# In every fourth step, half of the row maxima come from a + relu(b - a)

## Time and profile before

| | us |
|---|---|
| median of 3 runs (3239.01 to 3239.97) | 3239.01 |
| the profiled execution | 3237.97 |
| its span, first to last instruction | 3236.2 |

### The profile page before, as it was taken

How to read it: one execution, slowest core, us unless ns; L and a number is a source line. 1 busy time by engine, 2 the same in 40 slices (tenths; PEclk the granted TensorE clock), 3 DMA queues, 4 the chain that set the end, 5 groups by cost and what they waited for, 6 DMA issues and landing times.

```text
span 3236.2 us, 65472 instructions
## 1 busy us (share of the span) xinstructions
PE 2986.2 (92%) x19736; PEld 915.1 (28%) x19736; DVE 2807.7 (87%) x3214; ACT 2413.1 (75%) x4609; POOL 435.8 (13%) x672
## 2 busy tenths in 40 slices
PE   5888886699999999999999999999999999999999
PEld 3555553122222222222222222222222222222225
DVE  6666764899999999999999999999999999999972
ACT  4445353288888888888888888888888888888883
POOL 2545445000000000000000000000000000000000
PEclk9999998699999999999999999999999999999999
DMA  2222222011111111111111011111111111111125
GB/s 92 78 96 76 88 84 63 26 28 29 29 28 29 28 29 28 29 28 29 28 29 30 27 31 27 32 26 31 28 30 28 30 28 30 28 30 28 30 61 163
DMA packets 124612, 137.04 MB, mean 42 GB/s; under 512 B 43264, under 2 KB 103296, under 8 KB 124288
## 3 DMA queue, kind: packets, MB, share of 16 engines
q1 hardware_dynamic: 124288, 132.79, 15.0%
HBM read 88.15 MB, written 34.08 MB: 38 GB/s over the span
## 4 chain that ended last, share of the span: by engine, by line
PE 77%; DVE 7%; issue 7%; POOL 3%; ACT 3%; DMA 1%; DVEq 0%; SPq 0%; ACTq 0%; POOLq 0%
PE psum L679 31%; PE psum L695 29%; PE psum L644 14%; DVE row_max L1196 2%; PE psum L627 2%; ACT probs L805 1%; POOL qk_rot L834 1%; POOL parts L840 1%; PE psum L554 1%; PE psum L577 1%; POOL hT L846 1%; ACT silu L749 1%; DVE xn L977 1%; DVE y_blk L1117 1%; DVE rot_s L1095 0%
## 5 line engine op out<-in xcount | busy, mean ns | idle before, releaser
L1196 DVE TENSOR_REDUCE row_max<-psum 128x1 f32<-128x1024 f32 x2048 | 2402.7, 1218 | 166.0 <-PE psum L644 142.9
L805 ACT ACTIVATE probs<-psum 128x512 f32<-128x512 f32 x4096 | 2130.6, 602 | 407.9 <-PE psum L695 405.0
L695 PE MATMUL psum<-q_op,k_op 51*128 51x512 f16 x4096 | 1249.7, 387 | 42.2 <-ACT probs L805 20.2
L644 PE MATMUL psum<-k_op,q_op 48*128 48x512 f16 x4096 | 1047.0, 393 | 97.1 <-issue 43.8
L679 PE MATMUL psum<-probs,v_op 128*32 128x512 f32 x8192 | 1104.6, 611 | 8.3
L695 PEld LDWEIGHTS psum<-q_op,k_op 51*128 51x128 f16 x4096 | 314.5, 94 | 1359.0 <-ACT probs L805 1235.3
L915 POOL TENSOR_TENSOR acc_sb<-acc_sb,inv_rows 128x512 f32<-128x512 f32 x64 | 81.6, 1276 | 1841.4 <-DMA inv_rows<-inv_dram 1841.4
L644 PEld LDWEIGHTS psum<-k_op,q_op 48*128 48x128 f16 x4096 | 217.5, 94 | 389.9 <-DVE row_max L1196 302.5
L679 PEld LDWEIGHTS psum<-probs,v_op 128*32 128x32 f32 x8192 | 163.3, 108 | 262.3 <-issue 244.1
L742 ACT ACTIVATE parts<-qk_rot 128x512 f16<-128x512 f32 x64 | 40.3, 630 | 244.1 <-POOL qk_rot L834 244.1
L554 PE MATMUL psum<-xnT,w 128*128 128x512 f16 x768 | 184.6, 388 | 9.9 <-DVE h L1108 9.9
(11 more groups left out here) (102 smaller groups left out, 1019.1 us busy)
## 6 DMA issues: line engine op xcount, KB each, us to landing
qk_dram<-staged SPq DMA_DIRECT2D x64, 256.0 KB, 2.9
q_op<-qk_dram SPq DMA_DIRECT2D x128, 128.0 KB
k_op<-qk_dram SPq DMA_DIRECT2D x128, 128.0 KB
x_ln<-in_x SPq DMA_DIRECT2D x16, 512.0 KB, 3.5
x_res<-in_x SPq DMA_DIRECT2D x16, 512.0 KB, 4.2
y_dram<-y_blk SPq DMA_DIRECT2D x16, 512.0 KB, 3.1
k_op<-qk_dram SPq DMA_DIRECT2D x128, 64.0 KB
q_op<-qk_dram SPq DMA_DIRECT2D x128, 64.0 KB
```

The source lines that it names most:

```text
L644: mm = pe.matmul(bank(2 * half + j), q_op[r:r + ROWS, s, t * P:(t + 1) * P], k_op[r:r + ROWS, s, cols:cols + BANK], start=True, stop=True)
L695: pe.matmul(bank(b), k_op[r:e, h % SLOTS, t * P:(t + 1) * P], q_op[r:e, h % SLOTS, j * BANK:(j + 1) * BANK], start=True, stop=True).then_i ...
L805: nc.scalar.activation(probs[:, g2 % 2, j * BANK:(j + 1) * BANK], bank(b), ACT.Exp, scale=to_score).then_inc(s2_used, 1)
L1196: nc.vector.tensor_reduce(row_max[:, hl % 2, t, half:half + 1], psum[:, 2 * half * BANK:(2 * half + 2) * BANK], AX.X, ALU.max).then_inc(s1 ...
```

## The change

In some halves the maximum of 1024 scores is taken in another way. Let a and b be the two blocks of 512 columns. TensorE writes a into the first bank as before; into the second it accumulates b and then q times (-a's keys), that is b - a. ScalarE takes the positive part of b - a from PSUM into SBUF (`over`). VectorE then adds a and that block and takes the maximum, in one pass of 512 columns: max(a, b) = a + relu(b - a).

This is done for half 1 of the tiles t = 3, 7, 11 and 15 of heads 1 to 63, and for both halves of all tiles of head 0 (`diff_of`). GpSimd makes the negated keys per head (`negate`), before `split_max` of the head before. ScalarE's new operation stands ahead of the exps for half 0 and between exp j1 and exp j2 for half 1. VectorE no longer uses `run_steps`: its 1024 steps are written out.

```diff
+LOWEST = -3.0e38
+DIFF_EVERY = 4
+DIFF_AT = 3
...
+    k_neg = sb(sB, "k_neg", [P, 2, 2, BANK], F16)
+    over = sb(sB, "over", [P, 2, BANK])
...
+    DIFFS = TILES // DIFF_EVERY
+    def diff_of(c, half):
+        h, t = divmod(c, TILES)
+        if h == 0:
+            return 2 * c + half
+        if half == 1 and t % DIFF_EVERY == DIFF_AT and c < N1:
+            return 2 * TILES + DIFFS * (h - 1) + t // DIFF_EVERY
+        return None
+    def half_of(d):
+        if d < 2 * TILES:
+            return d
+        h, n = divmod(d - 2 * TILES, DIFFS)
+        return 2 * (TILES * (h + 1) + DIFF_EVERY * n + DIFF_AT) + 1
...
# TensorE, max_half
+            if diff_of(c, half) is not None:
+                pe.wait_ge(neg_ready, hl + 1 + SLOTS * i)
+                a = 2 * half * BANK
+                q_tile = q_op[HALF:HALF + ROWS, s, t * P:(t + 1) * P]
+                pe.matmul(bank(2 * half + 1), q_tile, k_op[HALF:HALF + ROWS, s, a + BANK:a + 2 * BANK], start=True, stop=False)
+                pe.matmul(bank(2 * half + 1), q_tile, k_neg[HALF:HALF + ROWS, hl % 2, half, :],
+                          start=False, stop=True).then_inc(diff_full, 1)
+                pe.matmul(bank(2 * half), q_op[0:ROWS, s, t * P:(t + 1) * P], k_op[0:ROWS, s, a:a + BANK],
+                          start=True, stop=True).then_inc(s1_full, 1)
+                return
...
# ScalarE, step
+            def positive_part(half):
+                d = diff_of(c, half)
+                if d is None:
+                    return
+                if d >= 2:
+                    act.wait_ge(s1_used, half_of(d - 2) + 1 + 2 * UNROLL * i)
+                act.wait_ge(diff_full, d + 1 + DIFFS * SLOTS * i)
+                nc.scalar.activation(over[:, d % 2, :], bank(2 * half + 1), ACT.Relu).then_inc(over_ready, 1)
...
+            positive_part(0)
             g2 = c - FIRST2
...
+            for j in range(4):
+                if j == 2:
+                    positive_part(1)
+                if 0 <= g2 < N1:
                     b = arrived(item)
...
# GpSimd
+        def negate(h):
+            pool.wait_ge(qk_loaded[h % SLOTS], 16 * QK_LOADS * (h // SLOTS + 1))
+            if h >= 2:
+                pool.wait_ge(s1_full, 2 * TILES * (h - 1))
+            halves = k_op[:, h % SLOTS, :].rearrange("p (a b n) -> p a b n", a=2, b=2)
+            first = 0 if h == 0 else 1
+            nc.gpsimd.tensor_scalar(k_neg[:, h % 2, first:2, :], halves[:, first:2, 0, :], -1.0, None,
+                                    ALU.mult).then_inc(neg_ready, 1)
+        negate(0)
         for h in range(HEADS):
             copy_v(h)
+            if h + 1 < HEADS:
+                negate(h + 1)
             split_max(h, h == 0)
...
# VectorE, step
+                    d = diff_of(c, half)
                     dve.wait_ge(s1_full, 2 * c + half + 1 + 2 * UNROLL * i)
+                    if d is not None:
+                        dve.wait_ge(over_ready, d + 1 + DIFFS * SLOTS * i)
+                        nc.vector.tensor_tensor_reduce(over[:, d % 2, :], bank(2 * half), over[:, d % 2, :], 1.0, LOWEST,
+                                                       ALU.add, ALU.max, row_max[:, hl % 2, t, half:half + 1]).then_inc(s1_used, 1)
+                        continue
...
-        run_steps(dve, step)
+        for c in range(STEPS_B):
+            step(c, 0)
```

More of the change, by code:

```diff
@@ L269, in layer_program @@
     stab_step = sem("stab_step")
+    neg_ready = sem("neg_ready")
+    diff_full = sem("diff_full")
+    over_ready = sem("over_ready")
     sums_moved = sem("sums_moved")
@@ L798, in step @@
                 item += STAB_ITEMS
+            positive_part(0)
             g2 = c - FIRST2
[L800 to L803, removed]
+            if 2 <= g2 < N1:
+                act.wait_ge(pv_done, g2 - 1 + UNROLL * i)
+            for j in range(4):
+                if j == 2:
+                    positive_part(1)
+                if 0 <= g2 < N1:
                     b = arrived(item)
```

## The result

| | before | after |
|---|---|---|
| median us (lowest to highest, 4 runs each) | 3239.01 (3237.21 to 3239.97) | 3313.82 (3302.04 to 3319.46) |
| profiled execution us | 3237.97 | 3319.46 |
| its span us, mean granted clock | 3236.2, 0.972 | 3317.7, 0.963 |

The ratio of the times is 1.0227, with a 95% interval of 1.0197 to 1.0257. The kernel became 75 us slower (64 to 83 by that interval). The forecast was 23 us slower with a range up to 3302, so the sign was right and the size was three times too small. The profiled execution after is the slowest of its four, and the four lie 17 us apart; what follows takes this one apart, so its parts add up to 81.5 and not to 75.

What follows compares the result with a forecast made beforehand. The prediction took a 2.39 us loop of TensorE and ScalarE, without VectorE, as the bound. 12.3 + 2.5 + 6.0 = 20.8 us, plus 2 for head 0, gave 3260.8 profiled, 3262 median; range 3241 to 3302.

Steps and rivals of the forecast that it cites:

- 0.60 + 0.06 + 0.31 + 1.00 + 0.42 = 2.39 ... there is no VectorE in it: Plain step: waits from exp j3 through j2, weigh_v and j3 to the next exp j3 make the whole 2.39 us period.
- the idle 0.20 before j2 hides it: TensorE, changed half: the extra matmul's 0.22 slot falls into free time before j2, leaving +0.02.
- +0.04: ScalarE, changed half: with the relu as fifth operation, the next exp j3 starts 2.43 after the last, against 2.39.
- The delay of the loop is D - 0.68 = +0.07: VectorE, changed half: the new pass of duration D, taken as 0.75, waits for the relu and delays the next step's j2.
- 0.05 for the semaphore: VectorE, changed half: assumed time from the relu's end to the start of the new pass, 0.05 us.
- the first two terms: Steps outside head 0 and loop edges: 175 x 0.07 + 63 x 0.04, that is 12.3 + 2.5 us.
- Nothing for ... VectorE's straight code: Loop edges: writing out VectorE's steps costs nothing, since its edge lies beside TensorE's branch of 4 us.
- +0.43: Behind each of 14 loop edges, at 1.2 GHz: t=11's changed half adds a matmul slot, 6.0 us in all.
- the middle is +1.0: Head 0's 32 changed halves: between +4.5 us at clock 0.50 and -2.4 at full clock.
- +1.1 ... at most double: Before head 0: GpSimd's negated keys, 1.0 us at the cast's rate plus 0.1 for semaphores, uncovered.
- The rival of a second instruction: VectorE's new pass: the maximum is written by a second instruction, D = 0.93, about 3295 us; chance 0.17, shared with other lateness.
- or as late for another reason (over 3280): Whole kernel: outcome over 3280 us, by a second instruction or equal lateness from another cause; chance 0.17.

Runs made afterwards that it cites:

- the two kernels where VectorE is not late: Changed kernel written out, head 0 as before, with the relu one ScalarE slot earlier (3189.88 us) or with VectorE's pass waiting for ScalarE alone (3187.75 us).
- The kernel with one wait: Against the written-out changed kernel with head 0 as before: the new pass waits for ScalarE alone, ScalarE waits for TensorE's results; 3187.75 us, ratio 0.9854.
- equal placement: Kernels before and after, both with the head of TensorE's loop at slot 8 of a 256-instruction block: before 3236.45 us, after 3284.46 us.

## Why the prediction was right in sign and wrong in size

- **"0.60 + 0.06 + 0.31 + 1.00 + 0.42 = 2.39 ... there is no VectorE in it": right.** Plain steps stay at 2.39, and 512 added passes cost nothing.
- **Extra matmul, "the idle 0.20 before j2 hides it": right**, cost 0.
- **Relu, "+0.04": right in kind, 0.057 measured** in the two kernels where VectorE is not late. The starts come a little closer than forecast (exp j3 at 1554.02, 2.40 after the one before, and not 2.43: +0.01); the rest, 0.048, is that the exp behind four others is recorded with 0.645 us and after an idle with 0.597.
- **"The delay of the loop is D - 0.68 = +0.07": the step that failed first.** D was 0.70 to the signal, less than the 0.75 assumed, and by the formula +0.02. But "0.05 for the semaphore" was 0.14, because the pass waits for two engines and the second wait is an instruction of its own; 0.02 more is the relu's 0.62. Measured +0.14 behind t=7, 11 and 15. For the three: 3 x 0.14 + 0.06 (t=3, where the output's copy hides the rest, as forecast) = 0.48 per head, x 62 = 29.8 us against the 14.8 of the first two terms. The kernel with one wait (2.447 instead of 2.53) shows the cause.
- **"Nothing for ... VectorE's straight code" and "+0.43" behind an edge: the largest failure.** The term 14 x 0.43 = 6.0 asked what the added instructions do in the cold steps, and for that the size was fair: +3.0 at equal placement. What was not asked is where the loop's code comes to lie once instructions are added to it and ahead of it. That costs 33 us in the profiled executions (27 by the medians), some two fifths of all that was lost, by a second stall of TensorE behind half 1 (1.7 to 2.3 us, 14 times) and a longer stretch at the lower clock: 0.50 is granted for 6.8 us at five edges and 10.2 at nine, where before it was 3.4 at five and 6.8 at nine. The earlier trace rows showed branches of 4 us, and the argument used them only as cover for others.
- **Head 0, "the middle is +1.0": the wrong end.** The clock stayed at its lower level of 1.2 GHz, a granted share of 0.50, and a half took 1.31, close to the 1.27 that had been worked out for it: +6.4. The row of a stretch (busy us of each engine, clock, DMA share, GB/s) shows TensorE busy 74% of the time, up from 53%, and no rise:

```profile
585.00:600.00 15.00, 11.15 (x36) 1.45 (x33) 7.76 (x23) 6.63 (x12) 1.49 (x1) 0.50 0.04 14
```

- **Negated keys, "+1.1 ... at most double": too low.** All engines of after at the start of stage B:

```profile
579.29 2.82 POOL L975 TENSOR_SCALAR k_neg<-k_op 128x1024 f16<-128x1024 f16 x1 [14.39 <-DMA k_op<-qk_dram]
...
582.25 0.58 PE L673 MATMUL psum<-k_op,q_op 48*128 48x512 f16 x1 [37.05 <-POOL k_neg L975]
```

  2.82 us, all uncovered: the cast from int32 to f32 was no model for a multiplication of f16. The further 2.6 of the +5.4 are not shown to be the change's; the start of head 0 moves by as much between kernels that have no such keys.
- **The end, +4.1: not forecast.** In the last head TensorE waits 2.43 us for the stabiliser, the split and transposed maxima (0.84 before), and behind this wait the clock is at 0.50 for 6.8 us, where weigh_v lasts 1.93 and not 1.07. Before, then after:

```profile
3143.53 0.60 PE L695 MATMUL psum<-q_op,k_op 51*128 51x512 f16 x3 [0.84 <-DMA q_op<-stabT]
...
3222.87 1.03 PE L733 MATMUL psum<-q_op,k_op 51*128 51x512 f16 x3 [2.43 <-DMA q_op<-stabT]
```

  The kernels with diff halves differ by as much among themselves here (the written-out one has none of it), so its cause stays open.

By the trace: 29.8 (forecast 14.8) + 35.8 (6.0) + head 0 and its keys 9.2 (2) + 6.7 not assigned to the change (0) = 81.5, against 22.8. Of the excess of 58.7, placement is 33, the second wait about 15 (186 steps x 0.083, the difference of 2.53 and 2.447), head 0 and its keys about 7, and the rest is 6.7 not assigned less the 3.0 by which the edges themselves came out cheaper than their forecast.

Of the signs that the forecast named, the plain step of 2.39, VectorE's idle time of 0.7 and ScalarE without idle time ahead of exp j3 came true. The step behind a diff half was 2.53 and not 2.43 to 2.46, and head 0 was off by more than 5 us. The rival of a second instruction had the instruction right and its price wrong. Its case, "or as late for another reason (over 3280)", is where the time came to lie. But with TensorE's loop at slot 8 the time is 3284.46, so 29 us of it are placement, which no rival had.

The Trainium skill, "Runtime: NRT & Kernel Launch", section "Instruction fetch mechanics", says that instructions come in blocks of 256, that a taken branch whose target isn't held forces a fetch before execution goes on, and that kernels for this reason do well to be written out. The runs agree: 69.5 us of edges before and 105.3 after, 1.8 and 1.6 written out. By that rule the 4.05 us of the earlier trace rows could have been read as a fetch, and where the code lies in its blocks as a rival of the forecast; that the second stall is a fetch too fits with its going by placement, but is not shown by itself.

## What to carry to other kernels

Work out the loop that closes on itself before lightening the busiest engine: at 87% busy VectorE had time to spare in every step, and giving it half the work of a pass in exchange for a wait on ScalarE made the step longer. Price each wait of an instruction by itself, and have one engine collect the others' signals where that engine has time. When instructions are added to a loop, compare its edges as well as its steps, and put the loop's head at the same slot (or write both kernels out) before a difference of 1% is put down to the computation.

## What the runs showed that was not expected

- Fourteen loop edges cost nearly as much as this change, and more than its computation (69.5 against 36.9 us): the kernel before takes 3173.29 us written out, 2.05% less, and 3197.29 with the branch announced.
- A second stall of 1.7 to 2.3 us (1015.28 + 0.42 to 1017.43 in the edge shown) can stand behind a branch that is itself shorter, and the profile puts it down to an engine that finished 5 us earlier.
- VectorE's second wait costs some 0.1 us (0.14 with two waits, 0.03 with one, from the relu's end to the pass).
- ScalarE's exp of 128x512 is recorded with 0.597 us after an idle and with 0.645 behind four others, though the starts stay 0.48 apart.
- GpSimd multiplies f16 in 2.82 us for 128x1024 and 1.49 for 128x512.
